# Attention: six of a batch's sixteen cache pages are asked for by GpSimd on its own queue, ten by SyncE

## The chip, the cores and the metric

The kernel runs on one core of one Trainium2 chip. The metric is the device time of one execution, in microseconds (us). TensorE multiplies matrices, VectorE (DVE), ScalarE (ACT) and GpSimd (POOL) work on tiles in SBUF, the on-chip memory of 128 partitions; SyncE (SP) issues DMAs, which 16 DMA engines carry out between HBM and SBUF. Each engine has its own stream of instructions, and they meet at semaphores.

## The reference

Input are 64 batches of 32 tokens with 512 features. Four residual layers follow one another. Layer 0 is attention over a paged cache: 32 query heads, 8 key heads of size 128, and for each batch 16 pages of 32 keys and values, drawn by a table from 64 pages. Layers 1 to 3 are a linear layer with routed low-rank experts and two with low-rank adapters. Cut to what matters here:

```python
q, k, v = x @ Wq.T, x @ Wk.T, x @ Wv.T              # 32, 8 and 8 heads of 128
q, k = rope(rmsnorm(q) * q_w, pos), rope(rmsnorm(k) * k_w, pos)
kc = k_cache[block_table].reshape(B, 512, 8, 128)   # 16 pages of 32 keys for each batch
vc = v_cache[block_table].reshape(B, 512, 8, 128)
k_all, v_all = concat([kc, k]), concat([vc, v])     # 512 + 32 = 544 keys
probs = softmax(where(valid, q @ k_all.T * SCALE, -1e30))
x = x + (probs @ v_all) @ Wo.T
x = x + moe_lora(x); x = x + lora2(x); x = x + lora3(x)
```

## The kernel before, in words

There are three stages. `project` (lines 226 to 739) makes queries, keys and values of all 2048 tokens and stores them in HBM (`q_spill`, `k_spill`, `v_spill`). `attend` (742 to 984) is the attention. `finish` (from 987) multiplies by Wo and does the other layers.

In `attend` a batch is 8 units (`HK`), 512 units in all; a unit is 128 rows of scores (4 heads of 32 tokens) against 544 keys. TensorE's stream (lines 935 to 982) goes in periods of two units: `score` of both (line 951), then `weigh_values` (line 971) of the two units of three periods before (`SUM_LAG = 3`). A batch is four periods. Batch b is scored in periods 4b to 4b+3, and its last value matmul is in period 4b+6. So the last value matmul of batch b-3 ends period 4b-6, and the first score of batch b begins period 4b; five periods lie between them. A value step alternates 72 and 64 matmuls. ScalarE and VectorE do the softmax between the two: mask and minimum (`lower_scores`, line 898), exponent (856), scaling (862), transposition into `p_t` (912). VectorE builds one mask for each batch (line 889). ScalarE copies a batch's result to `o_t` (868).

The keys and values of a batch lie in one of three buffers (`BUFS = 3`) of `kv`, which has 17 slots: 16 pages of 256 KB and the batch's own keys and values. Queries have two buffers. SyncE's stream (lines 794 to 830) does for each batch b from 3 on, in this order: it waits until the values of batch b-3 are summed (`summed`, line 807), since that frees the buffer; loads the sixteen pages (`load_pages`, lines 123 to 130); own keys (133), own values in four DMAs (137); waits until batch b-2 is scored (812); loads the queries (141); for b below 6 a part of Wo; waits for the copied result of batch b-3 and stores it (798). `load_pages` first reads the sixteen page numbers into registers of SyncE (line 125), then issues one DMA for each page; all of them and the own keys count on the buffer's semaphore `pages_in`.

TensorE waits at the first score of a batch (line 941) for `pages_in` and the queries (`q_in`), and for VectorE's `masked` (946).

GpSimd does little in this stage: in batches 9 to 24 it splits one slice of Wo for each batch into an upper and a lower part (`upper_weights`, line 839, and `lower_weights`, line 843), each after a wait for ScalarE's normalised weights (lines 846 and 848). Only `finish` reads them.

Of the kernel before, what the change touches and what calls it, by code (L numbers as in the profile page):

```python
# [67 lines left out]
def buf_of(b):  # L68

    return (b + BUFS - 1) % BUFS  # L70
# [12 lines left out]
def decoder(nc, x_t, x_rows, w_qkv, wo_t, q_norm_w, k_norm_w, inv_freq, kv_pages, block_table, seqlens,  # L83
            lang, slot2, slot3, w1_t, wr_a_t, b1_rows, w2_t, bias2, a2_rows, b2_rows, b3_rows, a3_rows, out):
    with ExitStack() as whole:
# [17 lines left out]
        with nc.Block() as block, ExitStack() as ctx:  # L103
# [16 lines left out]
            q_in = [sem("q_in0"), sem("q_in1")]  # L120
            v_own_in = [sem(f"v_own_in{i}") for i in range(BUFS)]

            def load_pages(sp, b):

                _, page = nc.values_load_multi_w_load_instructions(
                    pages[0:1, b * NPP:(b + 1) * NPP], engines=[mybir.EngineType.SP], min_val=0,
                    max_val=PAGES - 1, skip_runtime_bounds_check_because="the table names pages of the cache")
                for i in range(NPP):
                    sp.dma_start(kv[:, buf_of(b), i],
                                 kv_pages[bass.ds(page[i], 1)].rearrange("b d n -> (b d) n")).then_inc(pages_in[buf_of(b)], 16)  # L130

            def load_own_keys(sp, b):
                sp.dma_start(kv[:, buf_of(b), NPP, 0:VALUES], k_dram[b]).then_inc(pages_in[buf_of(b)], 16)
# [608 lines left out]
def attend(nc, block, sem, projected, copied, seq_f, pages, in_page_i, key_index, q_t, kv, pages_in, q_in, v_own_in, wo_early,  # L742
# [9 lines left out]
    QUAD = P // S  # L752
    SLOTS_P = 4
    SUM_LAG = 3

    with ExitStack() as ctx:
        def sb(name, shape, dt=F32):
# [16 lines left out]
        o_banks = [ps(f"o_bank{a}", [P, BANK]) for a in range(QUAD)]  # L774

        load_pages, load_own_keys, load_queries, load_own_values = loads
        own_unmasked = sem("own_unmasked")
        scored = sem("scored")
        masked_in = sem("mask_built")
# [14 lines left out]
        @block.sync  # L794
        def _(sp):
            def store(b):
                sp.wait_ge(o_out, (b + 1) * QUAD)
                sp.dma_start(o_dram[b], o_t[:, b % 2].rearrange("p g n -> p (g n)")).then_inc(o_stored[b % 2], 16)

            sp.wait_ge(projected, NSL * NT)  # L800
            load_pages(sp, 2)
            for b in range(2, B):
                if b == BUFS:
                    for i in range(2):
                        sp.wait_ge(stored[i], 16 * (NV + (NQ + NK) * NT) * (NT // QUARTER) // 2)
                if b >= BUFS:
                    sp.wait_ge(summed, 4 * (b - BUFS + 1))
                if b > 2:
                    load_pages(sp, b)
                load_own_keys(sp, b)  # L810
                load_own_values(sp, b)
                sp.wait_ge(scored, (b - 1) * HK)
                load_queries(sp, b)
                if b in WO_WITH:
                    h = WO_WITH[b]
                    sp.dma_start(wo_early[:, h:h + HS], wo_t[:, h:h + HS, :]).then_inc(wo_in, 16)
                if b >= BUFS:
                    store(b - BUFS)
            sp.wait_ge(summed, 4 * (B - 2))
            load_late(sp)  # L820
            store(B - 3)
            sp.wait_ge(summed, 4 * (B - 1))
            store(B - 2)
            sp.wait_ge(scored, UNITS)
            for par in range(2):
                sp.wait_ge(o_stored[par], 16 * TB // 2)
            for c in range(2):
                load_chunk(sp, 0, c)
            load_first(sp)
            store(B - 1)  # L830

        @block.gpsimd
        def _(pool):
            pool.wait_ge(projected, NSL * NT)

            def upper_weights(h):
                if h == 0:
                    pool.wait_ge(wo_in, 16 * (WO_EARLY // HS))
                nc.gpsimd.tensor_copy(hi_early[:, h], wo_early[:, h]).then_inc(hi_early_done, 1)

            def lower_weights(h):
                pool.wait_ge(hi_early_done, h + 1)
                nc.gpsimd.tensor_sub(lo_early[:, h], wo_early[:, h], hi_early[:, h].bitcast(F32)).then_inc(early_split, 1)

            for h in range(HI_EARLY):
                pool.wait_ge(normed, (SPLIT_FROM + h) * HK + 2)
                upper_weights(h)
                pool.wait_ge(normed, (SPLIT_FROM + h) * HK + 6)
                lower_weights(h)

        @block.scalar
        def _(act):
# [82 lines left out]
        @block.tensor  # L935
        def _(pe):
            def score(n):
                b, hh, r = n // HK, n % HK // REP, n % REP
                buf = buf_of(b)
                if n % HK == 0:  # L940
                    pe.wait_ge(pages_in[buf], 16 * (NPP + 1) * (b // BUFS + 1))
                    pe.wait_ge(q_in[b % 2], 16 * (b // 2 + 1))
                if n < 2:
                    pe.wait_ge(copied, NV * NT - 4 + 2 * n)
                else:
                    pe.wait_ge(masked, n - 1)
                for columns, slots in ((slice(BANK - CUT * PSIZE, BANK), slice(0, CUT)),
                                       (slice(BANK, BANK - CUT * PSIZE + KEYS), slice(CUT, NPP + 1))):
                    for a in range(QUAD):
                        g, rows = 2 * a + hh, slice(a * S, (a + 1) * S)  # L950
                        last = pe.matmul(s_banks[n % 2][rows, columns].rearrange("p (s t) -> p s t", t=PSIZE),  # L951
                                         q_t[:, b % 2, g, r * S:(r + 1) * S],
                                         kv[:, buf, slots, g * PSIZE:(g + 1) * PSIZE], start=True, stop=True)
                last.then_inc(scored, 1)

            def weigh_values(u):
                m, half = u // 2, u % 2
                b, hh = m // 2, m % 2
                buf = buf_of(b)
                if half == 0:  # L960
                    pe.wait_ge(turned, REP * (m + 1))
                    if m == 0:
                        pe.wait_ge(copied, NV * NT)
                elif hh == 0:
                    pe.wait_ge(v_own_in[buf], 16 * QUAD * (b // BUFS + 1))
                for c in range(CUT) if half == 0 else range(CUT, SLOTS):
                    for a in range(QUAD):
                        rows = slice(a * S, (a + 1) * S)
                        if hh == 0 and c == 0:
                            at_least(pe, o_out, (b - 1) * QUAD + a + 1)  # L970
                        last = pe.matmul(o_banks[a][:, hh * ROWS:(hh + 1) * ROWS],  # L971
                                         kv[rows, buf, c, VALUES + hh * HD:VALUES + (hh + 1) * HD],
                                         p_t[rows, m % 2, c].rearrange("p r s -> p (r s)"),
                                         start=hh == 0 and c == 0, stop=hh == 1 and c == SLOTS - 1)
                last.then_inc(summed, 1)

            for t in range(PERIODS + SUM_LAG):
                if t < PERIODS:
                    score(2 * t)
                    score(2 * t + 1)  # L980
                if t >= SUM_LAG:
                    weigh_values(t - SUM_LAG)

# [555 lines left out]
```

## Time and profile before

| what | value |
|---|---|
| median of 3 runs | 2220.04 us (2217.65 to 2234.28) |
| profiled execution | 2221.79 us, its span 2220.0 us |
| PE matmuls busy | 2152.6 us, 97% |
| PE weight loads busy | 1647.3 us, 74% |
| DVE busy | 1462.8 us, 66% |
| ACT busy | 1392.3 us, 63% |
| POOL busy | 220.3 us, 10% |
| DMA, SyncE's queue (q1) | 485.62 MB, 68.3% of 16 engines |
| DMA, instruction queues | 3.70 MB (q8) and 0.89 MB (q14) |
| chain of work that ended last | PE 94%, "issue" 2%, SyncE's queue 2%, DMA 1% |

Busy times are shares of the span from the first to the last instruction. Instructions that only issue DMAs, wait or load registers count as no engine's busy time. "Issue" is time in which an engine waited for nothing that the profile can name. A DMA's "landing" is when its semaphore has its last count. The share of a DMA queue is the time that its packets took, of 16 engines.

### The profile page before, as it was taken

Reading aid. Unit: us, or ns where it says so; the run is one execution under the profiler, and the core shown is the slowest. Engines: PE = TensorE matmul, PEld = TensorE weight load, DVE = VectorE, ACT = ScalarE, POOL = GpSimd, SP = SyncE. Lnnn points to the kernel's source line nnn. Section 1 sums busy time; section 2 is a strip of 40 time slices with the busy share of each in tenths; the row PEclk is TensorE's granted clock in tenths of the full one; section 3 lists DMA queues with packets and bytes.
Section 4 is the critical chain, followed back from the end, with each engine's and each line's share of the span. In section 5 each row is a group of like instructions: output and inputs, shape, how many; then the busy total and the mean of one; then the engine's idle time right before and its main releaser. Section 6 shows DMA issues by size and latency. Waiting matters only on the chain.

```text
span 2220.0 us, 77529 instructions
## 1 busy us (share of the span) xinstructions
PE 2152.6 (97%) x30576; PEld 1647.3 (74%) x30576; DVE 1462.8 (66%) x3642; ACT 1392.3 (63%) x4174; POOL 220.3 (10%) x208
## 2 busy tenths in 40 slices
PE   8999999999999999999999999999999999999998
PEld 6888888887666766667676676676777888888886
DVE  5799999994566766667676666666764433433433
ACT  4888888884677777777777777777773222222221
POOL 5211111110000111100000000000003101101101
PEclk9999999999999999999999999999999999999999
DMA  5455545548999999999999999999984333333331
GB/s 193 104 131 113 115 110 117 132 97 272 359 338 319 324 330 317 312 321 329 334 323 319 323 309 328 314 316 308 335 295 145 107 90 101 107 95 101 98 101 50
DMA packets 355010, 490.22 MB, mean 221 GB/s; under 512 B 58994, under 2 KB 191346, under 8 KB 351987
## 3 DMA queue, kind: packets, MB, share of 16 engines
q1 hardware_dynamic: 354674, 485.62, 68.3%
q8 instruction: 226, 3.70, 0.7%
q14 instruction: 110, 0.89, 0.1%
HBM read 397.37 MB, written 88.08 MB: 219 GB/s over the span
## 4 chain that ended last, share of the span: by engine, by line
PE 94%; issue 2%; SPq 2%; DMA 1%; DVE 1%; ACT 1%; ACTq 0%; DVEq 0%
PE o_bank L971 25%; PE s_bank L951 23%; PE acc L730 8%; PE acc L731 8%; PE acc L732 8%; PE proj L1408 5%; PE proj L1410 5%; PE proj L1409 5%; PE wide L1455 1%; PE wide L1450 1%; PE slim L1439 1%; PE wide L1451 1%; PE turn L1429 1%; PE slim L1437 1%; DMA kv<-k_spill 0%
## 5 line engine op out<-in xcount | busy, mean ns | idle before, releaser
L971 PEld LDWEIGHTS o_bank<-p_t,kv 32*128 32x128 f32 x17408 | 519.5, 187 | 134.0 <-issue 132.8
L898 DVE CUSTOM_DVE_ANT_0 probs<-s_bank,mask 128x544 f32<-128x544 f32 x512 | 370.7, 725 | 356.3 <-PE s_bank L951 356.3
L971 PE MATMUL o_bank<-p_t,kv 32*128 32x128 f32 x17408 | 574.8, 277 | 23.5 <-issue 22.7
L951 PE MATMUL s_bank<-kv,q_t 128*32 128x288 f32 (+1 forms) x8192 | 531.3, 397 | 22.7 <-issue 20.6
L856 ACT ACTIVATE probs<-probs,neg_max 128x544 f32<-128x544 f32 x512 | 383.4, 752 | 258.5 <-DVE neg_max L898 246.7
L951 PEld LDWEIGHTS s_bank<-kv,q_t 128*32 128x32 f32 x8192 | 247.7, 110 | 217.1 <-issue 32.4
L912 DVE STREAM_TRANSPOSE p_t<-probs 128x544 f32<-128x544 f32 x512 | 365.3, 731 | 0.4 <-ACT probs L862 0.4
L862 ACT ACTIVATE probs<-probs,inv_sum 128x544 f32<-128x544 f32 x512 | 356.8, 751 | 0.0
L730 PE MATMUL acc<-w_hi,x_hi 128*128 128x512 f32 x764 | 300.5, 393 | 0.0
L731 PE MATMUL acc<-w_lo,x_hi 128*128 128x512 f32 x764 | 300.1, 393 | 0.0
L732 PE MATMUL acc<-w_hi,x_lo 128*128 128x512 f32 x764 | 298.1, 390 | 0.0
L547 ACT ACTIVATE normed<-acc,kv 128x128 f32<-128x128 f32 x640 | 183.3, 373 | 54.4 <-DVE kv L670 53.9
L556 ACT ACTIVATE squares<-acc 128x128 f32<-128x128 f32 x640 | 170.5, 300 | 15.9 <-PE acc L732 15.5
L730 PEld LDWEIGHTS acc<-w_hi,x_hi 128*128 128x128 f32 x764 | 143.4, 188 | 37.4 <-ACT normed L547 5.7
L732 PEld LDWEIGHTS acc<-w_hi,x_lo 128*128 128x128 f32 x764 | 143.5, 188 | 31.6
L731 PEld LDWEIGHTS acc<-w_lo,x_hi 128*128 128x128 f32 x764 | 143.6, 188 | 29.4
L1219 ACT ACTIVATE low_t<-turn 128x128 fp32r<-128x128 f32 (+1 forms) x48 | 15.0, 313 | 229.9 <-PE turn L1459 229.9
L556 ACT ACTIVATION_READ_ACCUMULATOR squares<-acc 128x1 f32 x640 | 148.2, 232 | 0.0
L661 DVE TENSOR_TENSOR q_t<-normed,kv 128x256 f32<-128x256 f32 x320 | 130.2, 448 | 0.0
L189 DVE TENSOR_TENSOR o_lo<-raw,o_hi 128x1024 fp32r<-128x1024 f32 x64 | 83.9, 1311 | 67.8 <-ACT o_hi L182 67.5
L677 DVE TENSOR_TENSOR q_t<-part_s,q_t 128x512 f32<-128x512 f32 x160 | 118.8, 742 | 0.0
L652 DVE TENSOR_TENSOR part_s<-normed,kv 128x512 f32<-128x512 f32 x160 | 116.9, 731 | 1.8 <-ACT normed L547 1.7
(137 smaller groups left out, 2466.7 us busy)
## 6 DMA issues: line engine op xcount, KB each, us to landing
kv<-in_kv_pages SPq DMA_DIRECT2D x1024, 256.0 KB, 4.6
q_spill<-stage SPq DMA_DIRECT2D x512, 64.0 KB, 1.8
q_t<-q_spill SPq DMA_DIRECT2D x64, 512.0 KB, 5.8
o_spill<-o_t SPq DMA_DIRECT2D x64, 512.0 KB, 6.6
raw<-o_spill SPq DMA_DIRECT2D x64, 512.0 KB, 3.5
kv<-in_w_qkv SPq DMA_DIRECT2D x11, 1024.0 KB, 5.8
v_spill<-stage SPq DMA_DIRECT2D x8, 1024.0 KB, 7.1
k_spill<-stage SPq DMA_DIRECT2D x128, 64.0 KB, 1.8
```

The lines of the kernel that those rows point to most:

```text
L547: last = nc.scalar.activation(normed[:, i, h], acc_of(n)[:, h * HD:(h + 1) * HD], ACT.Copy, scale=rstd[:, i, h:h + 1])
L556: last = nc.scalar.activation(squares[:, i, h], acc_of(n)[:, h * HD:(h + 1) * HD], ACT.Square, accum_out=sumsq[:, i, h:h + 1])
L661: last = nc.vector.tensor_tensor(part_c[:, i, :, lo:lo + HALF], normed[:, i, :, hi:hi + HALF], cr[:, t, lo:lo + HALF].unsqueeze(1).broadca ...
L730: pe.matmul(bank, x_hi[:, c, toks], w_hi[:, s % 2, c], start=c == 0, stop=False)
L731: pe.matmul(bank, x_hi[:, c, toks], w_lo[:, s % 2, c], start=False, stop=False)
L732: last = pe.matmul(bank, x_lo[:, c, toks], w_hi[:, s % 2, c], start=False, stop=c == DC - 1)
L856: nc.scalar.activation(probs[:, i], probs[:, i], ACT.Exp, scale=-1.0, bias=neg_max[:, i:i + 1], accum_out=row_sum[:, i:i + 1]).then_inc(we ...
L862: nc.scalar.activation(probs[:, i], probs[:, i], ACT.Copy, scale=inv_sum[:, i:i + 1]).then_inc(normed, 1)
L898: nc.vector.tensor_tensor_reduce(out=probs[:, i], in0=s_run(n), in1=mask[:, b % 2], scale=-SCALE, scalar=3.0e38, op0=ALU.add, op1=ALU.min, ...
L912: nc.vector.transpose(p_t[:, m % 2, :, r], probs[:, n % SLOTS_P].rearrange("p (c e) -> p c e", e=S))\
L951: last = pe.matmul(s_banks[n % 2][rows, columns].rearrange("p (s t) -> p s t", t=PSIZE), q_t[:, b % 2, g, r * S:(r + 1) * S], kv[:, buf, s ...
L971: last = pe.matmul(o_banks[a][:, hh * ROWS:(hh + 1) * ROWS], kv[rows, buf, c, VALUES + hh * HD:VALUES + (hh + 1) * HD], p_t[rows, m % 2, c ...
```

## The change

`load_pages` gets the queue, the slots and the semaphore as arguments. For batches 0 to 2 SyncE still loads all sixteen pages. From batch 3 on SyncE loads slots 0 to 9, and GpSimd slots 10 to 15, in a loop of its own that waits for the same `summed` count, reads the six page numbers into its registers and issues six DMAs that count on new semaphores (`pool_pages_in`). The two halves of a Wo slice now follow the page loads of batches 9 to 24 without waits for the normalised weights. TensorE waits for both semaphores at the first score of a batch.

```diff
-            def load_pages(sp, b):
+            def load_pages(queue, b, slots=range(NPP), engine=mybir.EngineType.SP, landed=pages_in):
 
+                first = b * NPP + slots[0]
                 _, page = nc.values_load_multi_w_load_instructions(
-                    pages[0:1, b * NPP:(b + 1) * NPP], engines=[mybir.EngineType.SP], min_val=0,
+                    pages[0:1, first:first + len(slots)], engines=[engine], min_val=0,
                     max_val=PAGES - 1, skip_runtime_bounds_check_because="the table names pages of the cache")
-                for i in range(NPP):
-                    sp.dma_start(kv[:, buf_of(b), i],
-                                 kv_pages[bass.ds(page[i], 1)].rearrange("b d n -> (b d) n")).then_inc(pages_in[buf_of(b)], 16)
+                for i, slot in enumerate(slots):
+                    queue.dma_start(kv[:, buf_of(b), slot],
+                                    kv_pages[bass.ds(page[i], 1)].rearrange("b d n -> (b d) n")).then_inc(landed[buf_of(b)], 16)
...
+    ON_POOL = 6
...
+        pool_pages_in = [sem(f"pool_pages_in{i}") for i in range(BUFS)]
...
                 if b > 2:
-                    load_pages(sp, b)
+                    load_pages(sp, b, range(NPP - ON_POOL))
...
-            for h in range(HI_EARLY):
-                pool.wait_ge(normed, (SPLIT_FROM + h) * HK + 2)
-                upper_weights(h)
-                pool.wait_ge(normed, (SPLIT_FROM + h) * HK + 6)
-                lower_weights(h)
+            for b in range(BUFS, B):
+                pool.wait_ge(summed, 4 * (b - BUFS + 1))
+                load_pages(pool, b, range(NPP - ON_POOL, NPP), mybir.EngineType.Pool, pool_pages_in)
+                h = b - SPLIT_FROM
+                if 0 <= h < HI_EARLY:
+                    upper_weights(h)
+                    lower_weights(h)
...
                 if n % HK == 0:
-                    pe.wait_ge(pages_in[buf], 16 * (NPP + 1) * (b // BUFS + 1))
+                    pe.wait_ge(pages_in[buf], 16 * (NPP + 1 + (NPP + 1 - ON_POOL) * (b // BUFS)))
+                    at_least(pe, pool_pages_in[buf], 16 * ON_POOL * (b // BUFS))
                     pe.wait_ge(q_in[b % 2], 16 * (b // 2 + 1))
```

## Rows read from the trace of the kernel before

**Rows 1.** Busy time by stage: attention; stretch, its length, busy (count) by engine, clock, DMA.
```profile
core 0: us, PE busy (x) PEld busy (x) DVE busy (x) ACT busy (x) POOL busy (x), PEclk, DMA share, GB/s
541.50:1659.00 1117.50, 1071.55 (x25598) 767.09 (x25600) 757.16 (x2114) 825.18 (x1792) 30.37 (x32) 1.00 0.95 324
```

**Rows 2.** TensorE's timeline, 722 to 742 us: start, length, instruction.
```profile
722.57 2.04 PE L951 MATMUL s_bank<-kv,q_t 128*32 128x288 f32 x32
...
734.92 2.04 PE L951 MATMUL s_bank<-kv,q_t 128*32 128x288 f32 x32
...
738.89 2.04 PE L951 MATMUL s_bank<-kv,q_t 128*32 128x288 f32 x32
```

**Rows 3.** DMA from 600 to 1600 us: queue; issues, KB each, median us to landing.
```profile
q8 instruction: 181, 2.97, 1.2%
...
q_t<-q_spill SPq DMA_DIRECT2D x58, 512.0 KB, 5.8
o_spill<-o_t SPq DMA_DIRECT2D x58, 512.0 KB, 6.6
```

**Rows 4.** Waits from 600 to 1600 us: us in total, times, longest.
```profile
PE o_bank L971 <- issue: 18.5, 25, 2.5
PE s_bank L951 <- issue: 16.4, 14, 2.4
```

**Rows 5.** Timelines of TensorE and of SyncE's queue around 908 us; idle time in brackets.
```profile
903.99 2.29 PE L971 MATMUL o_bank<-p_t,kv 32*128 32x128 f32 x72
908.72 2.04 PE L951 MATMUL s_bank<-kv,q_t 128*32 128x288 f32 x32 [2.44 <-issue]
...
887.82 11.04 SPq L129 DMA_DIRECT2D kv<-in_kv_pages  x16
...
902.76 0.43 SPq L141 DMA_DIRECT2D q_t<-q_spill  x1
903.24 0.43 SPq L798 DMA_DIRECT2D o_spill<-o_t  x1
906.31 9.69 SPq L129 DMA_DIRECT2D kv<-in_kv_pages  x16
...
918.40 0.42 SPq L141 DMA_DIRECT2D q_t<-q_spill  x1
```

**Rows 6.** The tile of the queries, its one load of 902.8 us.
```profile
DMA to landing us min/median/max: 5.9/5.9/5.9
```

**Rows 7.** TensorE's timeline: waits in the middle of a run of scores.
```profile
700.48 1.12 PE L951 MATMUL s_bank<-kv,q_t 128*32 128x288 f32 x15 [0.57 <-issue]
...
823.08 1.51 PE L951 MATMUL s_bank<-kv,q_t 128*32 128x256 f32 x18 [1.94 <-issue]
...
1200.86 0.64 PE L951 MATMUL s_bank<-kv,q_t 128*32 128x256 f32 x8 [0.89 <-issue]
...
1280.87 1.51 PE L951 MATMUL s_bank<-kv,q_t 128*32 128x256 f32 x19 [0.28 <-issue]
```

**Rows 8.** A wait inside a value run; DMA, 592.4 to 592.8 us; two bursts of pages.
```profile
594.99 0.94 PE L971 MATMUL o_bank<-p_t,kv 32*128 32x128 f32 x20 [2.48 <-issue]
...
q8 instruction: 1, 0.02, 15.0%
...
591.31 4.66 SPq L129 DMA_DIRECT2D kv<-in_kv_pages  x8
...
818.50 4.75 SPq L129 DMA_DIRECT2D kv<-in_kv_pages  x8
```

**Rows 9.** SyncE: its waits, 600 to 1600 us; line 125; landing of the page DMAs.
```profile
SPq L125 <- PE o_bank L971: 89.2, 46, 5.7
SPq L141 <- PE s_bank L951: 5.6, 17, 0.5
...
L125 SPq TENSOR_LOAD <-pages x64: 967/1774/2992, 518.1 to 1613.8; - x64
...
DMA to landing us min/median/max: 2.6/4.6/8.8
```

**Rows 10.** Two stretches of the burst from 1010.39 us; columns as in Rows 1.
```profile
1010.40:1012.40 2.00, 2.00 (x62) 1.57 (x60) 1.43 (x6) 2.00 (x6) 0.00 (x0) 1.00 0.72 216
...
1021.40:1023.40 2.00, 2.00 (x68) 1.59 (x60) 1.81 (x6) 1.42 (x3) 0.00 (x0) 1.00 1.06 402
```

**Rows 11.** GpSimd's two operations of the stage and VectorE's mask: ns min/median/max.
```profile
L839 POOL CAST hi_early<-wo_early x16: 611/612/613, 705.7 to 966.1; 128x512 fp32r<-128x512 f32 x16
...
L843 POOL TENSOR_TENSOR lo_early<-wo_early,hi_early x16: 1279/1287/1292, 715.3 to 977.5; 128x512 fp32r<-128x512 f32 x16
...
L889 DVE TENSOR_SCALAR mask<-key_index,seq_f x64: 460/466/486, 541.5 to 1622.4; 128x512 f32<-128x512 f32 x64
```

## The prediction

> **What bounds the kernel now.** I read the profile in this order: busy time by stage, the waits of the attention stage, the timelines of TensorE and of SyncE's queue around one wait, then the landing times. The attention stage takes 1117.5 us, half of the span, with TensorE's matmuls busy for 1071.55 us of it, its clock granted in full (1.00, the 2.4 GHz level), and the DMA engines at 0.95 [rows 1]. The projection before it and the layers after it load no pages, so the change can only act in this stage.
>
> Without a disturbance a batch costs TensorE 16.32 us: four periods of scores and values from 722.57 to 738.89 [rows 2]. Between 600 and 1600 us the queries of 58 batches were loaded [rows 3]; 58 x 16.32 = 946.6, so 53.4 us of these 1000 were lost. TensorE's idle time there is 18.5 + 16.4 us, all put down to "issue" [rows 4], so about 18 us more is hidden in matmuls that stand a little farther apart. "Issue" names no cause; the timelines show two.
>
> First, **queries that land late**. In the batch whose first score starts at 908.72 after 2.44 us of idle, SyncE issued sixteen pages from 887.82 on in 11.04 us, then own keys, own values, and only at 902.76 the queries [rows 5]. These took 5.9 us to land [rows 6]: 908.66, and TensorE started 0.06 us later. Of the fourteen waits of score matmuls in this stretch (16.4 us, [rows 4]) four stand in the middle of a run of scores and can't be a batch's data: 0.57 + 1.94 + 0.89 + 0.28 = 3.7 us [rows 7]. The other ten, 12.7 us, stand at a batch's first score, as that at 908.72 does.
>
> Second, **instructions that arrive late**. At 594.99 TensorE resumes in the middle of a run of value matmuls, where no wait stands in the program, after 2.48 us; a packet of the instruction queue had started in the 0.4 us around 592.6 [rows 8]. There were 181 such packets of 16 KB in 1000 us [rows 3], about three a batch. This second kind is what is left: 53.4 - 12.7 = 40.7 us.
>
> **The change, part by part.** (1) SyncE issues ten pages in place of sixteen for the 61 batches from 3 on. Sixteen took 9.69 us in the burst from 906.31 [rows 5], 0.61 each, so its own keys, values, queries and the store of an old batch all go out 6 x 0.61 = 3.6 us earlier. The queries' own waits don't eat that: SyncE's wait for scores cost 5.6 us in 17 times [rows 9], and those scores are made in the first period of the burst. SyncE's late starts go as well: in the burst from 887.82 it was busy until 903.67 and issued the next page at 906.31 [rows 5]; with 3.6 us less of issue it will be waiting for TensorE at every batch, as it now is at 46 of 58 [rows 9].
>
> (2) When do queries land? In the burst from 906.31 they were issued at 918.40, 12.1 us in, and with some 5.8 us to land [rows 3] arrive 18 us in. They can't overtake the work ahead: sixteen pages, keys, values and the queries are 5.0 MB. At the 402 GB/s that the rings reach late in a burst, where the first 2 us move 216 [rows 10], that is 12.4 us, plus 3 of latency: 15.4. At the stage's mean of 324 [rows 1] it is 15.4 plus 3, no gain. Two rings fill sooner than one, and that early low rate is what I expect to rise; I take 1 to 2.6 us earlier. The window is five periods, 5 x 4.08 = 20.4 us from the last value matmul of batch b-3 to the first score of b. SyncE needs 1.0 us at least for the page numbers [rows 9], so today's margin is 20.4 - 1.0 - 18 = 1.4 us, used up by a late start or a slow issue. With 1 to 2.6 more and no late start, nearly all ten waits go: -12.7 x 61/58 = -13.4, and some 0.6 us for waits under the 0.15 us that the profile shows: **-14 us**.
>
> (3) GpSimd waits for the same matmuls, loads six page numbers and issues six DMAs. The trace has no DMA of GpSimd's. From below: SyncE's 0.33 us for the instruction; from above: GpSimd's dearest operation in this stage, 1.29 us [rows 11]. I take the upper one, being its own engine's: six in 7.7 us, the last out 8.7 us after the wait, landed by the longest landing seen for a page, 8.8 us [rows 9], at 17.5: inside 20.4. Behind these DMAs on its engine stand only the cast and the subtraction of a weight slice in 16 batches, 0.61 + 1.29 us [rows 11]; nobody needs them before the last stage, and GpSimd is idle otherwise: 0 us. They lose their two waits for normalised weights: 0 too.
>
> (4) TensorE gets one more semaphore wait at 61 batch starts. It has three there now, and at 734.92, a batch's first score, it doesn't idle [rows 2]: 0, at most the usual 0.15 us below which the profile shows no gap, 9 us in all, if the sequencer were not ahead.
>
> (5) The instruction packets. The third ring could delay them, or the old store's earlier end could free them: between -20 and +39 us, worked out under the rivals; I take 0, since the same bytes pass in the same 16 us.
>
> The DMA descriptors of GpSimd are written by software. DVE could hold that up: its only operation here of the simple copying kind is the mask, 0.47 us once a batch [rows 11], so I take 0. The Trainium skill (SBUF — State Buffer, "SBUF: two separate sides") says that while VectorE runs a 2-port operation GpSimd cannot write descriptors, and (section "A bandwidth-pool intuition that's wrong (but worth ruling out)") that a DMA of some 0.6 us then takes 3.1. By that, applied to all six, they would take 18.6 us and come late; no run here shows it yet.
>
> **Sum.** The profiled execution took 2221.79 us (span 2220.0), 1.75 over the runs' median of 2220.04, inside their spread. 2221.8 - 14 = 2207.8; I write 2207.
>
> **Rivals.**
> *A, the forecast*: 0.50.
> *B, no gain*: the engines are the bound. For it: share 0.95 [rows 1], pages landing no faster than they are issued. Then queries land where they do and only the late starts go, a few us: 2218. Against it: 216 against 402 GB/s within one burst [rows 10]. 0.15. The Trainium skill (DMA: Bandwidth & Descriptors, "Issuing engines are not separate DMA queues") states this case's rule: DMAs from several engines share the 16 DMA engines, and only issue time is saved.
> *C, instructions also come sooner*: the store is issued at 903.24 with 6.6 us to land [rows 3, 5], so it still runs when the next burst starts at 906.31; two of the longest instruction waits, 2.48 and 1.94 us, end 3.7 and 4.6 us after a burst's first page, at 591.31 and 818.50 [rows 7, 8]. If the store is out of the way, I put half of the 40.7 us at stake: 2208 - 20 = 2188. 0.16.
> *D, instructions come later, slower than before*: each DMA engine has one more ring between two turns of the instruction ring, for six pages in sixteen, and its software-made packets may be long. 190 fetches in the stage (181 x 61/58): 14/190 = 0.07 us more for each undoes the gain, 0.19 us gives over 1% more. At 0.2: 2208 + 38 = 2246. Against: fetch packets take 1.2% of 16 engines [rows 3], 0.012 x 16 x 1000 / 181 = 1.06 us each, so the transfer itself is short beside the waits. 0.14.
> *E, GpSimd's pages are late*: it decides from 2.4 us a DMA, (20.4 - 1.0 - 5)/6; at 3.1 each the last page comes 4.2 us late, 61 times: 2208 + 256 = 2464. 0.05.
>
> About 1% is what a measurement of this kernel can tell from no change. Faster by over 1% (below 2198) is C and the low tail of A, 0.16 + 0.11; slower (over 2242) is most of D, and E, 0.17; the rest 0.56. The range 2187 to 2247 holds A, B, C and D's centre.
>
> **What would show it.** A: no idle at any batch's first score, SyncE's issue of ten pages in some 6 us, queries issued some 8.4 us into a burst, their landing over 2 us ahead of the first score; SyncE waiting for values at every batch. B: the queries' time to land grows by as much as they are issued earlier, ten waits remain. C and D: TensorE's idle in the middle of runs, 18.5 + 3.7 us now, falls under 12 or rises over 35. E: idle at first scores with GpSimd's pages landing just before. The prediction is wrong above all if a GpSimd DMA costs over 2.4 us, or if the instruction packets' delay, which the trace shows only in its effects, moves by more than 0.1 us each.

## The result, and the profile after

| | before | after |
|---|---|---|
| median, 4 runs each on one chip | 2220.73 us | 2292.87 us (2288.96 to 2298.98) |
| ratio | 1 | **1.0324** (95% interval 1.028 to 1.0367) |
| span of the profiled execution | 2220.0 us | 2287.1 us |
| attention stage | 1117.50 us | 1184.80 us |

The change costs 72 us; 2207 was forecast, with 2247 as the upper end. Of the 67.1 us between the two spans the attention stage has 67.3, so the other stages are out of it. The busy times and queues on the profile's first page:

```profile
span 2287.1 us, 77637 instructions
...
PE 2180.4 (95%) x30576; PEld 1656.9 (72%) x30576; DVE 1460.2 (64%) x3642; ACT 1393.8 (61%) x4174; POOL 416.3 (18%) x574
...
q1 hardware_dynamic: 301970, 389.65, 53.6%
q0 software_dynamic: 29280, 95.97, 11.6%
q8 instruction: 227, 3.72, 0.7%
...
PE 93%; issue 4%; SPq 1%; DMA 1%; ACT 0%; DVE 0%; ACTq 0%; DVEq 0%
```

No engine has more to do except GpSimd, whose 366 DMA instructions (197 us) do count as busy, and TensorE is still the chain's 93%; "issue" in the chain went from 2% to 4%. The attention stage as a window (columns as in [rows 1]):

```profile
542.30:1727.10 1184.80, 1097.51 (x25602) 775.17 (x25601) 757.51 (x2115) 827.03 (x1792) 227.67 (x398) 0.99 0.88 306
```

TensorE idles for 87.3 us of it (1184.80 - 1097.51) against 45.9 in [rows 1]; 26 us more stand in busy time, as the same matmuls lie farther apart and some run at a lower clock (last section). The DMA engines moved the same bytes in more time, 306 GB/s against 324: they didn't become the limit of the whole. The waits from 600 to 1600 us (us in total, times, longest), as in [rows 4, 9]:

```profile
PE o_bank L977 <- issue: 57.0, 56, 2.5
...
PE s_bank L957 <- issue: 12.4, 19, 1.5
...
SPq L126 <- PE o_bank L977: 374.5, 54, 10.6
```

Waits in value runs tripled from 18.5 to 57.0 us in 54 batches in place of 58. Of the 67 in the stage 62 stand past the first eight matmuls of a run, where the program has no wait. SyncE now waits 374.5 us for values, at every batch: it is far ahead. The DMAs of the same stretch (queue; issues, KB, median us to landing), as in [rows 3]:

```profile
q8 instruction: 170, 2.79, 1.1%
...
kv<-in_kv_pages SPq DMA_DIRECT2D x540, 256.0 KB, 7.6
kv<-in_kv_pages POOLq DMA_DIRECT2D x324, 256.0 KB, 6.5
q_t<-q_spill SPq DMA_DIRECT2D x55, 512.0 KB, 8.5
o_spill<-o_t SPq DMA_DIRECT2D x55, 512.0 KB, 9.3
```

**Every DMA takes longer to land**: a SyncE page 7.6 us (4.6 in [rows 9]), queries 8.5 us (5.8). The instruction packets themselves don't take longer: 0.011 x 16 x 1000 / 170 = 1.04 us each, as before (1.06). One burst, on SyncE, GpSimd and TensorE:

```profile
1013.47 7.04 SPq L130 DMA_DIRECT2D kv<-in_kv_pages  x10
...
1023.62 0.42 SPq L142 DMA_DIRECT2D q_t<-q_spill  x1
```
```profile
1014.39 3.46 POOL L130 DMA_DIRECT2D kv<-in_kv_pages  x6 [12.88 <-issue]
```
```profile
1014.21 1.26 PE L977 MATMUL o_bank<-p_t,kv 32*128 32x128 f32 x33
1016.61 1.39 PE L977 MATMUL o_bank<-p_t,kv 32*128 32x128 f32 x39 [1.14 <-issue]
...
1024.21 0.50 PE L977 MATMUL o_bank<-p_t,kv 32*128 32x128 f32 x8 [2.46 <-issue]
...
1030.70 1.12 PE L957 MATMUL s_bank<-kv,q_t 128*32 128x288 f32 x16 [0.75 <-issue]
```

Sixteen pages are asked for in 7.0 us where one queue took 9.69 [rows 5]. The queries, issued 10.15 us into the burst and landed 7.5 us later, are there at 1031.1, 2.7 us ahead of the batch's first score at 1033.75. But TensorE stops three times meanwhile, each time in the middle of a run. The DMA view of the 0.4 us from 1021.6 and from 1014.1 has one packet of the instruction queue each, some 2.3 to 2.6 us ahead of the end of the second stop and of the first, as in [rows 8]:

```profile
q8 instruction: 1, 0.02, 14.2%
```
```profile
q8 instruction: 1, 0.02, 16.6%
```

How full the 16 engines are in each 2 us of a burst (last two columns: share, GB/s), after from 1013.48 and before, the burst of [rows 10]:

```profile
1013.48:1015.48 2.00, 1.99 (x49) 1.39 (x42) 1.76 (x5) 2.00 (x6) 1.04 (x2) 1.00 0.62 171
1015.48:1017.48 2.00, 0.87 (x29) 0.87 (x32) 1.09 (x4) 2.00 (x6) 1.81 (x5) 1.00 0.99 352
1017.48:1019.48 2.00, 2.00 (x46) 1.26 (x43) 0.22 (x1) 0.09 (x1) 0.37 (x1) 1.00 0.93 301
1019.48:1021.48 2.00, 2.00 (x68) 1.59 (x59) 1.84 (x6) 1.41 (x3) 0.00 (x0) 1.00 1.04 391
```
```profile
1012.40:1014.40 2.00, 2.00 (x48) 1.27 (x44) 1.24 (x3) 1.05 (x2) 0.00 (x0) 1.00 0.73 222
1014.40:1016.40 2.00, 2.00 (x64) 1.57 (x61) 2.00 (x7) 1.96 (x6) 0.00 (x0) 1.00 0.76 266
1016.40:1018.40 2.00, 2.00 (x50) 1.28 (x46) 1.27 (x4) 1.08 (x3) 0.00 (x0) 1.00 0.82 280
1018.40:1020.40 2.00, 2.00 (x68) 1.65 (x64) 1.58 (x6) 1.93 (x6) 0.00 (x0) 1.00 1.01 347
```

In this pair of bursts the engines run at 0.72 to 0.82 for 8 us with one queue and are full after 2 us with two. The pair isn't typical. The mean share over all 61 bursts, in the first four slices of 2 us, is 0.76, 0.88, 0.95 and 0.97 before and 0.53, 0.91, 0.97 and 1.02 after, so the engines aren't full much sooner. What does differ is how much data is in flight, asked for and not landed, summed from the issue and landing times of the stage's DMAs: 1.47 MB on average before, 2.02 MB after, and over 2 MB in 3% of the stage before, in 53% after.

### The profile page after: what moved, and what is told of

The parts are those of the page before. It is cut to its first block, busy times and chain, and to the rows that moved or that the text cites. A ratio compares the mean times of both kernels' runs of the same rounds, so it can differ in the third digit from the quotient of the medians.

```text
span 2287.1 us, 77637 instructions
## 1 busy us (share of the span) xinstructions
PE 2180.4 (95%) x30576; PEld 1656.9 (72%) x30576; DVE 1460.2 (64%) x3642; ACT 1393.8 (61%) x4174; POOL 416.3 (18%) x574
## 3 DMA queue, kind: packets, MB, share of 16 engines
q0 software_dynamic: 29280, 95.97, 11.6%
## 4 chain that ended last, share of the span: by engine, by line
PE 93%; issue 4%; SPq 1%; DMA 1%; ACT 0%; DVE 0%; ACTq 0%; DVEq 0%
PE o_bank L977 25%; PE s_bank L957 23%; PE acc L731 8%; PE acc L733 8%; PE acc L732 7%; PE proj L1414 5%; PE proj L1416 5%; PE proj L1415 5%; PE wide L1456 1%; PE wide L1457 1%; PE wide L1461 1%; PE slim L1445 1%; PE turn L1435 1%; PE slim L1443 1%; DMA kv<-k_spill 0%
## 5 line engine op out<-in xcount | busy, mean ns | idle before, releaser
L977 PEld LDWEIGHTS o_bank<-p_t,kv 32*128 32x128 f32 x17408 | 528.4, 187 | 184.7 <-issue 183.6
L977 PE MATMUL o_bank<-p_t,kv 32*128 32x128 f32 x17408 | 589.6, 278 | 67.2 <-issue 66.8
L957 PE MATMUL s_bank<-kv,q_t 128*32 128x288 f32 (+1 forms) x8192 | 542.9, 399 | 20.1 <-issue 18.2
L130 POOL DMA_DIRECT2D kv<-in_kv_pages x366 | 197.3, 539 | 974.7 <-issue 962.0
L190 DVE TENSOR_TENSOR o_lo<-raw,o_hi 128x1024 fp32r<-128x1024 f32 x64 | 82.1, 1283 | 67.1 <-ACT o_hi L183 66.9
```

Source lines behind the costliest of these rows:

```text
L130: queue.dma_start(kv[:, buf_of(b), slot], kv_pages[bass.ds(page[i], 1)].rearrange("b d n -> (b d) n")).then_inc(landed[buf_of(b)], 16)
L977: last = pe.matmul(o_banks[a][:, hh * ROWS:(hh + 1) * ROWS], kv[rows, buf, c, VALUES + hh * HD:VALUES + (hh + 1) * HD], p_t[rows, m % 2, c ...
```

## The experiments

All are compared with the kernel before on the same chip (its medians: 2222.05 for e1 to e4, 2220.88 for e5 to e8, 2221.47 for f9 to f11, 2223.09 for g12). The idle times are all gaps of over 0.15 us in TensorE's timeline of the attention stage, split by place: **at a batch's first score** (where the program waits for data) or **mid-run** (anywhere else). The last column counts the mid-run gaps that end 2.0 to 2.8 us after the last 16 KB instruction packet started; by chance some 14% of the gaps would. Of 90 mid-run gaps after the change 87 stand inside a run, 3 at its start. SyncE's pages are 256 KB a DMA, in e5 and f9 512 KB.

| kernel | median us | ratio (95%) | mid-run us | first score us | SyncE's page lands, us | after a packet |
|---|---|---|---|---|---|---|
| before | 2220.7 | 1 | 28.1 | 16.7 | 4.6 | 34 of 36 |
| after | 2292.9 | 1.0324 (1.028 to 1.0367) | 82.8 | 3.7 | 7.6 | 88 of 90 |
| e1 one queue, queries earlier | 2201.9 | 0.9908 (0.989 to 0.9926) | 22.7 | 3.8 | 4.6 | 31 of 33 |
| e2 second queue is ScalarE's | 2275.7 | 1.0253 (1.0226 to 1.0281) | 70.1 | 2.9 | 7.1 | 82 of 88 |
| e3 GpSimd starts after six pages | 2258.7 | 1.0151 (1.0114 to 1.0188) | 34.9 | 39.0 | 4.4 | 43 of 45 |
| e4 GpSimd's DMAs carry 4 KB | 2178.6 | 0.9808 (0.9779 to 0.9837) | 13.6 | 3.5 | 4.3 | 18 of 21 |
| e5 one queue, 8 DMAs of 512 KB | 2284.4 | 1.0276 (1.0236 to 1.0317) | 79.0 | 1.9 | 7.5 | 94 of 96 |
| e6 two queues, both paced | 2344.3 | 1.0538 (1.0489 to 1.0586) | 13.8 | 112.7 | 4.4 | 17 of 19 |
| e7 one queue, 4 in flight, pairs | 2532.8 | 1.1395 (1.135 to 1.144) | 2.7 | 260.3 | 3.4 | 2 of 4 |
| e8 GpSimd has 2 pages, not 6 | 2233.0 | 1.0053 (1.0028 to 1.0078) | 41.1 | 4.0 | 5.1 | 58 of 60 |
| f9 e5 with 6 pages in flight | 2262.6 | 1.02 (1.0158 to 1.0242) | 15.2 | 58.9 | 5.6 | 23 of 26 |
| f10 e1 with 6 in flight | 2262.3 | 1.0209 (1.0163 to 1.0256) | 6.0 | 73.7 | 4.6 | 7 of 9 |
| f11 e1 with 8 in flight | 2210.4 | 0.9962 (0.9935 to 0.9989) | 17.1 | 11.3 | 5.3 | 24 of 27 |
| g12 after, with more instructions | 2405.2 | 1.0812 (1.077 to 1.0855) | 144.7 | 3.5 | 7.7 | 111 of 114 |

**e1: the gain without the second queue.** From the kernel before:

```diff
                 load_own_keys(sp, b)
-                load_own_values(sp, b)
                 sp.wait_ge(scored, (b - 1) * HK)
                 load_queries(sp, b)
+                load_own_values(sp, b)
```

> The kernel before, all sixteen pages on SyncE's queue, but the queries are asked for ahead of the four DMAs of own values. It tests the term of the prediction that was to bring the gain, with one queue alone. Theory (the ten waits at a batch's first score, 12.7 us in 1000, end with the queries' landing, and the changed kernel lost its time elsewhere): queries go out about 2 us earlier, the waits at first scores fall from 16.7 us in the whole stage to under 4, 2205 to 2212 us. Rival (the waits only gave the instruction packets time to catch up): the waits at first scores go but idle time in the middle of runs grows from 28 us by as much, 2216 to 2224 us. Rival (the engines are the bound, queries land when they did): 2220 us with the waits where they were.

Measured: 2201.86 us, 0.9908. The queries now go out ahead of the own values. The burst on SyncE (from 1006.02), and the waits from 540 to 1990 us:

```profile
1006.02 8.74 SPq L129 DMA_DIRECT2D kv<-in_kv_pages  x16
...
1015.32 0.46 SPq L141 DMA_DIRECT2D q_t<-q_spill  x1
1015.82 2.93 SPq L137 DMA_DIRECT2D kv<-v_spill  x4
```
```profile
PE o_bank L971 <- issue: 16.6, 23, 1.7
...
PE s_bank L951 <- issue: 8.5, 10, 3.5
```

The waits at first scores fell from 16.7 to 3.8 us, as in the changed kernel, with pages still landing in 4.6 us and mid-run idle at 22.7. So late queries were a real loss and are curable by order alone; the time is 3 us under the range expected. What is left at first scores, here and after the change, is nearly all one wait of 3.5 to 3.7 us at batch 1, whose loads neither kernel changes. The queries went out 10.3 us into a burst (median of 61) in place of 12.6.

**e2: another kind of queue.** From the changed kernel: ScalarE's hardware queue asks for the six pages, fixed ones.

```diff
             for b in range(BUFS, B):
-                pool.wait_ge(summed, 4 * (b - BUFS + 1))
-                load_pages(pool, b, range(NPP - ON_POOL, NPP), mybir.EngineType.Pool, pool_pages_in)
...
+            def load_fixed_pages(act, b):
+                for slot in range(NPP - ON_POOL, NPP) if b < B else ():
+                    act.dma_start(kv[:, buf_of(b), slot], kv_page(slot)).then_inc(pool_pages_in[buf_of(b)], 16)
...
                     evacuate(done // 4 - 1)
+                    load_fixed_pages(act, done // 4 - 1 + BUFS)
```

> The changed kernel, but slots 10 to 15 are asked for by ScalarE on its hardware queue, right behind the copy of the result of batch b-3, and not by GpSimd. The page numbers are fixed (10 to 15) in place of the table's, so its output differs; bytes and shapes are the same. Theory 1 (a second data ring that has work makes TensorE's instruction packets wait, whoever makes its descriptors): idle time in the middle of runs stays near the changed kernel's 83 us, 2280 to 2300 us. Theory 2 (it is GpSimd's descriptors: written by software, in packets of 4096 bytes where SyncE's are 2048): it falls back to about 28 us and the queries' waits stay away, 2205 to 2225 us, of which up to 10 us may be ScalarE's six issues. Theory 3 (more bytes in flight, through any queue): as theory 1.

Measured: 2275.73 us, mid-run idle 70.1 us, landing 7.1 us. Waits from 540 to 1990 us and the queue from 600 to 1600:

```profile
PE o_bank L981 <- issue: 49.6, 59, 2.3
PE s_bank L961 <- issue: 21.1, 25, 2.9
```
```profile
q10 hardware_dynamic: 47527, 86.54, 25.7%
```

Without GpSimd and without a software-made packet three quarters of the added mid-run idle are there ((70.1 - 28.1) / (82.8 - 28.1) = 0.77). Packets that software makes are not the main cause. The last quarter may be theirs, or come from another time of asking: ScalarE asks once it has copied the result.

**e3: the second queue starts later.** From the changed kernel: the first six pages count on a semaphore of their own, and GpSimd waits for them.

```diff
             for b in range(BUFS, B):
-                pool.wait_ge(summed, 4 * (b - BUFS + 1))
+                pool.wait_ge(first_in[buf_of(b)], 16 * 6 * (b // BUFS))
```

> The changed kernel, but GpSimd waits until the first six of SyncE's ten pages of the same batch have landed before it asks for its own six, so the two queues overlap less and fewer bytes are in flight. Theory 3 (bytes in flight): idle in the middle of runs falls from 83 us to under 55, 2245 to 2265 us. Theory 2 (GpSimd's descriptors themselves): it stays at 75 to 90 us, 2285 to 2300 us. Theory 1 (two rings with work at once): in between, 60 to 75 us. If the six pages now come late, idle shows at first scores (1 batch-first wait in the changed kernel now).

Measured: 2258.65 us. Mid-run idle is down to 34.9 us and pages land in 4.4 us, but the batch's last pages are late: 39.0 us at first scores. Half of the one loss goes (2258.7 against 2292.9 us), and another comes in its place.

**e4: the second queue without its bytes.** From the changed kernel, each of GpSimd's six DMAs loads 8 columns of its page and no more:

```diff
+                cols = slice(0, PAGE if len(slots) >= NPP - 6 else TINY)
                 for i, slot in enumerate(slots):
-                    queue.dma_start(kv[:, buf_of(b), slot],
+                    queue.dma_start(kv[:, buf_of(b), slot, cols],
...
```

> The changed kernel, but GpSimd's six DMAs of a batch carry 8 numbers a partition (4 KB) in place of 512 (256 KB); so 1.5 MB of a batch's 5.5 MB are not loaded and the output differs. The number of software-made DMAs stays. Theory 2 in its first form (making and fetching software descriptors disturbs the instruction packets): idle in the middle of runs stays above 60 us, 2260 to 2290 us. Theories 1 and 3, and theory 2 in its second form (it is the 4096-byte packets): it falls to 5 to 25 us, since the engines carry a quarter less and the second ring is nearly empty, 2185 to 2205 us.

Measured: 2178.59 us, 0.9808, a little faster than any theory had it; mid-run idle 13.6 us. GpSimd issues as many DMAs a batch, but each is 32 packets in place of 80 (11328 in 354 DMAs from 600 to 1600 us), with 1.47 MB in place of 86:

```profile
q0 software_dynamic: 11328, 1.47, 2.2%
...
kv<-in_kv_pages POOLq DMA_DIRECT2D x354, 4.0 KB, 4.2
```

So a third queue and the work of issuing don't bring the loss by themselves; it needs the bytes. A small cost of the queue could still hide behind the 37% fewer page bytes, which also make 2178.6 no candidate.

**e5: one queue, filled faster.** From the kernel before: pages in pairs (`WIDE = 2`), fixed ones, on SyncE alone.

```diff
-                for i in range(NPP):
-                    sp.dma_start(kv[:, buf_of(b), i],
-                                 kv_pages[bass.ds(page[i], 1)].rearrange("b d n -> (b d) n")).then_inc(pages_in[buf_of(b)], 16)
+                for i in range(0, NPP, WIDE):
+                    sp.dma_start(kv[:, buf_of(b), i:i + WIDE],
+                                 kv_pages[i:i + WIDE].rearrange("b d n -> d b n")).then_inc(pages_in[buf_of(b)], 16)
```

> The kernel before, SyncE's queue alone, but its sixteen pages are asked for in eight DMAs of two neighbouring pages (512 KB each), with fixed page numbers 0 to 15 and so another output. The bytes are the same, the one queue is filled at up to twice the rate, and the queries go out some 5 us earlier. Theory 3 (bytes in flight, however many queues): pages and queries take 7 us and more to land in place of 4.6 and 5.8, and idle time in the middle of runs rises from 28 us to 50 us or more; 2235 to 2290 us. Theory 1 (a second data ring with work, whatever the bytes): one ring, so the idle stays at 20 to 30 us, and the queries' waits go: 2198 to 2212 us.

Measured: 2284.43 us, 1.0276, mid-run idle 79.0 us. The burst is asked for in 5.45 us:

```profile
1011.46 5.45 SPq L130 DMA_DIRECT2D kv<-in_kv_pages  x8
```
```profile
PE o_bank L972 <- issue: 61.4, 68, 2.1
PE s_bank L952 <- issue: 18.0, 27, 1.9
```

(The waits are those from 540 to 1990 us.) This is nearly the loss of the changed kernel **with no second queue at all**. A second queue isn't needed for it; how fast a burst is asked for is what e2, e5 and the changed kernel have in common. On average 1.93, 2.22 and 2.02 MB are in flight in them, 1.47 before. No run tells what fixed pages do by themselves, in e2 and e5; f9 has those of e5 and little mid-run idle.

**e6, e7: both faults at once?** e6, from the changed kernel, and e7, from e1, let a queue run only so far ahead of what has landed (e6: four pages on SyncE's and two on GpSimd's; e7: four). e7's core:

```diff
                 for i in range(NPP):
+                    if b > 2 and i >= IN_FLIGHT and i % GROUP == 0:
+                        sp.wait_ge(group_in[buf_of(b)][(i - IN_FLIGHT) // GROUP], 16 * GROUP * (b // BUFS + 1))
```

> The changed kernel with both queues kept short: pages count on semaphores in pairs; SyncE asks for pair p once its pair p-2 has landed (at most four of its pages in flight), GpSimd once its pair p-1 has (at most two). At most 1.5 MB of pages are in flight, as in the kernel before. Theory 3 (bytes in flight): idle in the middle of runs falls from 83 us to 35 or less; if the pages aren't late, 2200 to 2225 us. Theory 1 (two rings with work): it stays over 60 us, 2265 us and more.

> The kernel before with queries ahead of own values (2201.9 us) and, besides, SyncE's pages kept to four in flight, in pairs. Theory 3 (bytes in flight): the 22.7 us of idle left in the middle of runs fall to under 15, 2185 to 2198 us, unless the queries land late again. Theory 1: one ring before and after, so nothing changes there, 2198 to 2206 us, or slower if pages come late.

Measured: 2344.26 and 2532.76 us. Mid-run idle did fall, to 13.8 and 2.7 us. The data then came too late, by far more than I had expected; the waits from 540 to 1990 us, e6 then e7:

```profile
PE s_bank L970 <- DMA kv<-in_kv_pages: 63.2, 22, 5.2
PE s_bank L970 <- DMA q_t<-q_spill: 49.5, 20, 6.5
...
PE o_bank L990 <- issue: 9.3, 14, 1.8
```
```profile
PE s_bank L958 <- DMA q_t<-q_spill: 260.3, 62, 11.0
...
PE o_bank L978 <- issue: 1.2, 2, 0.7
```

In e7's burst from 1003.20 SyncE was busy with the sixteen pages for 16.63 us (9.69 in [rows 5]) and issued the queries 17.16 us in; with the median of 5.4 us to land they are there after 22.6 us, past the window of 20.4. So the two kernels show low mid-run idle together with late data, and no gain.

**e8: a smaller dose.** From the changed kernel, `ON_POOL = 2` in place of 6.

> The changed kernel with two pages on GpSimd's queue, fourteen on SyncE's. Theory 1 (ring with work): the second ring has work for about a third of the time that it has with six, so a third of the added idle: 40 to 50 us in the middle of runs; with part of the queries' waits gone 2225 to 2245 us. Theory 3 (bytes in flight): the two pages add 0.5 MB for a short time: 30 to 40 us of idle, 2210 to 2225 us.

Measured: 2232.95 us, 1.0053, mid-run idle 41.1 us, landing 5.1 us. Both lie between before (28.1 us, 4.6) and after (82.8, 7.6), in order: the loss grows with the share of the second queue. By their numbers this run is Theory 1's: idle and time lie in its ranges (40 to 50 us, 2225 to 2245), just outside those of Theory 3 (30 to 40, 2210 to 2225). On average 1.59 MB are in flight. So e5 shows that one queue is enough for the loss, but not that a second one with work adds nothing of its own.

**f9, f10, f11: milder pacing.** f9 is e5 with at most six pages in flight; f10 and f11 are e1 with six and with eight (the e11 of g12's text is f11).

> The kernel with pairs of fixed pages in one DMA (2284 us, 79 us of idle in the middle of runs), but SyncE asks for pair p only once pair p-3 has landed: the same eight large DMAs on one queue, at most six pages in flight. If bytes in flight are the cause and not the size or the number of DMAs: idle in the middle of runs falls to 15 to 35 us; 2200 to 2235 us if the data isn't late (idle at first scores tells). If the size of a DMA or its burst is the cause: it stays over 60 us.

> The kernel before with queries ahead of own values (2201.9 us), SyncE's pages kept to six in flight, each page with a semaphore of its own. Before it had about seven in flight (4.5 us to land, one issued each 0.6 us). If bytes in flight set the late instruction packets: idle in the middle of runs falls from 22.7 us to 8 to 16 us. The price is a later last page: if the queries still land in time 2188 to 2200 us; with waits at first scores again 2205 to 2240 us.

> The same with eight in flight: the limit seldom acts. Bytes in flight: 18 to 23 us in the middle of runs, no waits at first scores, 2196 to 2206 us. It also prices the semaphores: sixteen more waits of TensorE at each batch's start; if they cost anything, this is slower than 2202 us by it.

Measured: 2262.57, 2262.3 and 2210.4 us. In f9 mid-run idle is 15.2 us against e5's 79.0 with the same DMAs, so large DMAs don't bring it by themselves; it speaks for the bytes in flight, under the caution below. But again queries come late (f10, waits from 540 to 1990 us):

```profile
PE s_bank L958 <- DMA q_t<-q_spill: 72.4, 50, 3.9
```

All three are slower than expected, f9 and f10 by late data. f11 has 17.1 us of mid-run idle and 11.3 at first scores, where none was expected, and loses to e1 (2210.4 against 2201.9). Part of that is the price of its sixteen more waits on TensorE at a batch's start: the undisturbed value run ahead of them takes 2.42 us in place of 2.22, 0.2 us a batch, some 12 us in all. A caution: where TensorE waits for data at the first score, its instructions have time to catch up, so a part of the low mid-run idle of e3, e6, e7, f9 and f10 may come from that and not from the pacing.

**g12: is mid-run idle really missing instructions?** From the changed kernel: waits that are satisfied long before, 128 a batch, put into TensorE's stream. Half of them ride on a matmul's own instruction; the trace has 3904 more instructions, 64 a batch and not the 128 of the text below.

```diff
+                        for _ in range(2 if n >= 24 else 0):
+                            pe.wait_ge(copied, NV * NT)
```

> The changed kernel with 128 more instructions for TensorE's queue in each batch from 3 on: after each score matmul two waits for a count that was reached long before. The waits hold nothing up by themselves and sit in the score runs, where a matmul takes twice as long as among the values; e11 priced sixteen such waits at 0.2 us a batch, so 128 cost at most 1.6 us a batch, 98 us, if none is hidden. If the idle time in the middle of runs is TensorE waiting for packets of instructions: the packets of queue 8 in 1000 us rise from 170 towards 190, and the idle rises from 83 us to over 100. If that idle time has another cause (matmuls held by the memory, say): it stays at 75 to 90 us, and only the spacing inside score runs may grow.

Measured: 2405.24 us, 1.0812; mid-run idle 144.7 us against 82.8. An undisturbed score run still takes 2.04 us, so the waits themselves are hidden. Waits from 600 to 1600 us:

```profile
PE s_bank L957 <- issue: 56.7, 41, 3.3
...
PE o_bank L979 <- issue: 56.4, 46, 2.4
```

Idle in score runs, where the new instructions stand, rose from 12.4 to 56.7 us, and 111 of 114 gaps end 2.0 to 2.8 us after a packet starts. Packets per 1000 us did not rise as expected (166 against 170), since the stage got slower; in the whole stage they did, 216 against 200. So queue 8 carries TensorE's instructions, and more of them to bring means more idle with the same data: mid-run idle is the supply of instructions. Why 8% more packets bring 75% more idle isn't shown. The rest of the 112 us lost to the changed kernel is in part the clock: 1.2 GHz was granted for 61 us of the stage, for 14 us in the changed kernel.

**What follows.** The kernel that beats both is e1, 2201.86 us: 0.9% under before, 4.0% under the changed kernel.

## Why the prediction was wrong

**Step (5) failed**, the one that took 0 for the instruction packets "since the same bytes pass in the same 16 us". The bytes are the same, but with two queues they are asked for sooner and more of them wait: 2.02 MB in flight in place of 1.47, and pages take 7.6 us to land in place of 4.6. More instruction packets then come late: 88 mid-run gaps follow one in place of 34, of some 200 packets in the stage, and their mean length went from 0.78 to 0.92 us. When a packet was asked for no view shows; that it starts late is inferred from the gaps, which end some 2.45 us after its start in either kernel. The loss of the stage, against 240 periods of undisturbed length, went from 60.0 to 126.2 us, with the first scores' gain of 13.0 already in it: 79 us for some 190 packets, 0.42 us each. Mid-run idle carries 54.7 of it; the rest is in matmuls that stand farther apart, and a little in the clock (last section).

The other steps, in order. **(1)** Right: in the median of 61 bursts the pages were issued in 6.3 us in place of 9.8, and the queries went out 9.2 us into a burst in place of 12.6, 3.4 us earlier against the 3.6 forecast (the burst shown above, with 7.04 and 10.15 us, is a slow one). SyncE waits for values at every batch, as said. **(2)** Right in its result, in part by luck. Waits at first scores fell from 16.7 to 3.7 us: -13.0 against -13.4 forecast. But the queries didn't land sooner by a fuller start of the burst: they take 8.5 us in place of 5.8, which eats most of the 3.4 us, and they land only some 0.8 us sooner after a burst's first page. The burst itself starts 0.9 us sooner after the last value matmul (1.2 us in place of 2.1), and the window got 1.0 us longer on average, as TensorE itself lost time in it. Together that is the queries' slack to the first score, which rose from a median of 1.0 to 3.8 us. The 3 us of latency in the prediction's sum of 15.4 stand in no row; the shortest landing of a page in [rows 9] is 2.6. That late queries were the cause of these waits is shown by e1, which has the same gain from the order alone. **(3)** Right: GpSimd's six DMAs cost 0.54 us each at a cadence of 0.58 (I took 1.29, the upper bound), and its pages land in 6.5 us, the last of a batch at least 7 us ahead of the first score. Nothing behind them was late. The Trainium skill's rule that VectorE can hold up descriptor writing (SBUF — State Buffer, "SBUF: two separate sides") was not put to the test here: of VectorE's operations the prediction counted only the mask as such a one, and none of the 366 DMAs ran within 2 us of one. Beside the other operations of VectorE, busy for 64% of the span, the longest of GpSimd's DMAs took 0.72 us, so the 3.1 us was never seen. **(4)** Right: no idle of its own at batch starts. Sixteen more such waits are worth 0.2 us (f11), so one is within the bound given.

Of the rivals, E fell with step (3). B's rule, that more issuing engines add no DMA engines and save issue time only, holds here, 306 GB/s in the stage against 324 and issue 3.4 us shorter (the Trainium skill, DMA: Bandwidth & Descriptors, "Issuing engines are not separate DMA queues"), but it ends at no gain and says nothing of a loss. **D had the right kind of loss, a cause that isn't needed for it, and too small a size.** Its sign was mid-run idle over 35 us; it is 69.4 from 600 to 1600 us, and 0.42 us a packet where it priced 0.2. Of its cause, one more ring in the turn and long packets made by software, e2 loses 2.5% without the software, and e5 loses 2.8% without a further queue, against 3.2%; e4 has both with next to no bytes and doesn't lose. That the further ring adds something (e8) isn't excluded. [Rows 8] had the price: waits of 2.5 us behind one late packet, against which 0.2 us was no bound.

**What stays open.** Why an instruction packet starts late when much data is queued, inside the DMA engines, the traces don't show. That the engines are full isn't enough for it: of the packets that start behind 2 us at a share of 1.02 or more, 12 of 68 were followed by a gap before and 58 of 83 after. Bytes in flight fit better but don't order all kernels either: f11 has 1.63 MB, pages landing in 5.3 us and 17.1 us of mid-run idle, e8 1.59 MB, 5.1 us and 41.1. What is shown is that asking for a burst faster brings the loss, by a second queue or without one, and that the loss is in the supply of instructions.

## What to carry to other kernels

Where TensorE's program is long enough to be streamed beside the data (here three packets of 16 KB a batch), a short data queue has a worth of its own: before a change that asks for data faster, look for "issue" waits in the middle of matmul runs and at the landing times, and price a deeper queue by those waits. When one transfer is late, first move it ahead in its own queue (e1, one line) before giving the others a queue of their own. A cap on what is in flight traded instruction waits for data waits: it helped a little where the uncapped kernel was slow (f9 1.02 against e5's 1.0276, the intervals just meeting; e3 1.0151 against 1.0324, by a later start of the second queue), but not always there (e6 1.0538), and no capped kernel beat e1.

## What the runs showed of the hardware beyond that

An idle of TensorE may cost twice. After 1.98 us of idle in the changed kernel the granted clock fell and the next score run took 3.73 us in place of 2.04 (timeline; then windows, columns as in [rows 1]):

```profile
1066.08 0.93 PE L977 MATMUL o_bank<-p_t,kv 32*128 32x128 f32 x19 [1.98 <-issue]
1066.94 3.73 PE L957 MATMUL s_bank<-kv,q_t 128*32 128x288 f32 x32
```
```profile
1064.00:1068.00 4.00, 2.02 (x33) 1.27 (x34) 0.64 (x2) 1.42 (x4) 0.00 (x0) 0.88 1.05 341
1068.00:1072.00 4.00, 4.00 (x76) 2.30 (x72) 1.88 (x5) 1.22 (x3) 0.00 (x0) 0.69 0.30 120
```

The mean granted clock was 0.88 and 0.69 there, so part of these stretches ran at the 1.2 GHz level. That the idle brought the clock down isn't shown: after the 2.46 us that end at 1024.21 it stayed at 1.00 (windows 1021.48:1023.48 and 1023.48:1025.48). Between 560 and 1700 us four stretches of 20 us in the changed kernel are below 1.00 (0.95, 0.91, 0.91, 0.91), in the kernel before one (0.91). Over the whole stage the lower level was granted for 13.6 us, before for 6.8, so it explains at most some 3 us of the 67.

GpSimd's queue moves a page in 64 packets of 4096 bytes and 16 of 4 bytes (29280 for 366 pages), SyncE's and ScalarE's in 128 of 2048 and 16 of 4. With next to no data in them (e4) GpSimd's DMAs did no harm of their own.
